# Attention and expert layer on one core: two heads for each exponential and each maximum, and attention by tokens through transpositions

## The reference

```python
qkv = x @ W_qkv.T + b_qkv                     # 32 x 256 tokens, H = 16 heads, hs = 8
att = jnp.einsum('bthd,bshd->bhts', q, k) / math.sqrt(hs)
att_prob = jax.nn.softmax(att, axis=-1)
att_v = jnp.einsum('bhts,bshd->bthd', att_prob, v)
x = _layernorm(x + att_v @ W_out.T + b_out)
...
x = _layernorm(x + _L0_ffn_ref(x, ...))       # 8 experts, top 2, and a shared one
```

## Time and profile before

| | |
|---|---|
| median of 3 runs | 873.24 us (871.66 to 875.74) |
| the profiled execution | 874.22 us, span 872.4 us |
| PE, PE weight load busy | 91%, 56% |
| DVE, ACT, POOL busy | 81%, 64%, 61% |
| mean granted TensorE clock | 0.98 |

### The profile page before, as it was taken

How to read it: one execution, slowest core, us unless ns; L and a number is a source line. 1 busy time by engine, 2 the same in 40 slices (tenths; PEclk the granted TensorE clock), 3 DMA queues, 4 the chain that set the end, 5 groups by cost and what they waited for, 6 DMA issues and landing times.

```text
span 872.4 us, 21905 instructions
## 1 busy us (share of the span) xinstructions
PE 792.0 (91%) x6356; PEld 487.8 (56%) x6356; DVE 710.5 (81%) x1430; ACT 557.5 (64%) x1128; POOL 528.2 (61%) x684
## 2 busy tenths in 40 slices
PE   2688999999999999999999689999999899999994
PEld 1234555555555555555554557666666566666662
DVE  5576988898889989889987398888888888887885
ACT  1146887777778877877778346655555555556652
POOL 3446756656657667566533357666666676666664
PEclk9997999999999999999999799999999999999997
DMA  5634555555655655555420541444444544433430
GB/s 151 187 100 117 134 167 149 144 160 134 161 145 133 177 140 133 172 137 145 135 64 27 142 120 53 121 121 122 121 120 120 120 120 120 120 115 103 121 96 24
DMA packets 201643, 108.84 MB, mean 125 GB/s; under 512 B 10496, under 2 KB 201088, under 8 KB 201600
## 3 DMA queue, kind: packets, MB, share of 16 engines
q1 hardware_dynamic: 200048, 105.88, 45.0%
q10 hardware_dynamic: 1552, 2.44, 1.0%
HBM read 73.94 MB, written 33.82 MB: 124 GB/s over the span
## 4 chain that ended last, share of the span: by engine, by line
PE 50%; DVE 16%; issue 13%; POOL 9%; DMA 7%; ACT 2%; DVEq 1%; SPq 1%; POOLq 0%; ACTq 0%
PE bank L721 11%; DVE negmax L999 8%; PE bank L693 7%; PE bank L706 6%; DMA probs<-route_dram 6%; PE bank L823 4%; PE bank L728 3%; POOL place L507 3%; PE bank L729 3%; DVE k_stack L1073 3%; PE bank L730 3%; PE bank L803 2%; POOL rstd L516 2%; PE bank L887 2%; PE bank L783 2%
## 5 line engine op out<-in xcount | busy, mean ns | idle before, releaser
L999 DVE TENSOR_REDUCE negmax<-bank 128x2 f32<-128x512 f32 x512 | 321.3, 680 | 50.5 <-PE bank L706 46.3
L555 ACT ACTIVATE probs<-bank 128x512 f32<-128x512 f32 x512 | 292.2, 604 | 94.9 <-PE bank L693 93.9
L706 PE MATMUL bank<-k_stack,q_stack 48*128 48x256 bf16 x1024 | 168.9, 284 | 12.3 <-DVE negmax L999 5.4
L693 PE MATMUL bank<-q_stack,k_stack 50*128 50x256 bf16 x1024 | 168.1, 276 | 6.0 <-ACT probs L555 4.8
L728 PE MATMUL bank<-x_hi,hi_w 128*128 128x512 f32 x288 | 137.8, 479 | 11.3 <-DVE k_stack L1073 8.6
L721 PE MATMUL bank<-probs,v_aug 128*32 128x256 f32 x2048 | 138.8, 389 | 0.4 <-ACT attT L566 0.4
L693 PEld LDWEIGHTS bank<-q_stack,k_stack 50*128 50x128 bf16 x1024 | 75.5, 95 | 98.1 <-ACT probs L555 62.7
L1063 DVE TENSOR_TENSOR k_stack<-bank,probs 128x512 f32<-128x512 f32 x128 | 87.6, 685 | 44.4 <-DMA probs<-route_dram 26.2
L729 PE MATMUL bank<-x_hi,lo_w 128*128 128x512 f32 x288 | 115.4, 401 | 0.0
L730 PE MATMUL bank<-x_lo,hi_w 128*128 128x512 f32 x288 | 115.2, 400 | 0.0
L507 POOL TENSOR_TENSOR k_stack<-k_stack,probs 128x512 f32<-128x512 f32 x48 | 62.2, 1296 | 81.2 <-DVE k_stack L1073 73.4
(11 more groups left out here) (111 smaller groups left out, 1395.4 us busy)
## 6 DMA issues: line engine op xcount, KB each, us to landing
probs<-route_dram SPq DMA_DIRECT2D x128, 256.0 KB, 5.8
q_stack<-q_parts_dram SPq DMA_DIRECT2D x64, 192.0 KB, 3.2
k_stack<-k_parts_dram SPq DMA_DIRECT2D x64, 192.0 KB, 4.0
k_parts_dram<-k_parts SPq DMA_DIRECT2D x32, 192.0 KB, 2.0
q_parts_dram<-q_parts SPq DMA_DIRECT2D x32, 192.0 KB, 2.0
xT_sb<-xT SPq DMA_DIRECT2D x32, 128.0 KB, 2.1
k_parts_dram<-k_parts SPq DMA_DIRECT2D x32, 128.0 KB, 1.9
q_parts_dram<-q_parts SPq DMA_DIRECT2D x32, 128.0 KB, 2.0
```

The lines of the kernel that those rows point to most:

```text
L555: nc.scalar.activation(probs[h][:], score_ps[BANK[h]][:].rearrange("p (j t) -> p j t", j=NT), ACT.Exp).then_inc(exp_done, 1)
L693: mm = pe.matmul(score_ps[BANK[h]][:, j * T:(j + 1) * T], k_stack[b.ring][first:last, h // 2, j * P:(j + 1) * P], q_stack[b.ring][first:la ...
L706: mm = pe.matmul(max_ps[BANK[h]][:, i * T:(i + 1) * T], q_stack[b.ring][first:last, h // 2, i * P:(i + 1) * P], k_stack[b.ring][first:last ...
L999: nc.vector.tensor_reduce(negmax[b.ring % 2][:, :, column], max_ps[BANK[h]][:].rearrange("p (i s) -> p i s", i=NT), AX_X, ALU.max, negate= ...
```

## The change

Three edits in the attention part.

1. The S scores of two neighbouring heads go to one tile of two neighbouring banks, and ACT takes one exponential of 1024 values for both heads. There is one such tile (score_ps is twos[2]), where three banks took turns before. S matmuls of a pair wait, at its first head, until the exponentials of all pairs before it are done.
2. The M scores of two neighbouring heads go to another such tile, and DVE takes one reduction of 1024 values for both. There are two such tiles, in turn; the M matmuls of a pair wait for the reduction two pairs before.
3. The four matmuls of 72 columns that turn the sums to rows by tokens become four transpositions of 128 columns. POOL builds, at the start, an identity with its columns in another order (used_first), so that the used columns come first. A later transposition writes over the unused columns of the one before it.

```diff
-        probs = [sb(f"probs{r}", [P, NT, T]) for r in range(H)]
+        two_probs = [sb(f"two_probs{r}", [P, 2, NT, T]) for r in range(PAIRS)]
+        probs = [two[:, n] for two in two_probs for n in range(2)]
...
-        max_ps, score_ps, av_ps, misc = banks[0:3], banks[3:6], banks[6], banks[7]
+        twos = [ctx.enter_context(nc.psum_tensor(f"two_banks{n}", [P, 2, 512], F32)) for n in range(3)]
+        max_ps, score_ps, av_ps, misc = twos[0:2], twos[2], banks[6], banks[7]
...
+            pool.tensor_copy(used_first[:, 0:4 * W].rearrange("p (g w) -> p g w", w=W), columns[:, :, 0:W]).then_inc(consts_set, 1)
+            pool.tensor_copy(used_first[:, 4 * W:P].rearrange("p (g w) -> p g w", g=4), columns[:, :, W:32]).then_inc(consts_set, 1)
...
-                    if b.live:
-                        act_e.wait_ge(score_mm, b.count(H, h + 1))
+                    if b.live and h % 2 == 0:
+                        act_e.wait_ge(score_mm, b.count(PAIRS, h // 2 + 1))
                         if h % 4 == 0 and b.later(1):
                             act_e.wait_ge(av_mm, b.count(4, h // 4 - 3))
-                        nc.scalar.activation(probs[h][:], score_ps[BANK[h]][:].rearrange("p (j t) -> p j t", j=NT), ACT.Exp).then_inc(exp_done, 1)
+                        nc.scalar.activation(two_probs[h // 2][:].rearrange("p h j t -> p (h j t)"), score_ps[:].rearrange("p h t -> p (h t)"),
+                                             ACT.Exp).then_inc(exp_done, 1)
...
-                if j == 0 and (b.later(1) or h >= BACK[h]):
-                    pe.wait_ge(exp_done, b.count(H, h + 1 - BACK[h]))
+                if j == 0 and h % 2 == 0 and (b.later(1) or h):
+                    pe.wait_ge(exp_done, b.count(PAIRS, h // 2))
...
-                if j == NT - 1:
+                if j == NT - 1 and h % 2:
                     mm.then_inc(score_mm, 1)
...
-                if i == 0 and (b.later(1) or h >= BACK[h]):
-                    pe.wait_ge(max_red, b.count(H, h + 1 - BACK[h]))
+                if i == 0 and h % 2 == 0 and (b.later(1) or h >= 4):
+                    pe.wait_ge(max_red, b.count(PAIRS, h // 2 - 1))
...
-                                mm = pe.matmul(tok_ps[:, (2 * i + half) * 4 * W:(2 * i + half + 1) * 4 * W],
-                                               attT[:, half, i * P:(i + 1) * P], used, start=True, stop=True)
+                                mm = pe.transpose(misc[:, first:first + P], attT[:, half, i * P:(i + 1) * P], used_first[:])
...
-                        nc.vector.tensor_reduce(negmax[b.ring % 2][:, :, column], max_ps[BANK[h]][:].rearrange("p (i s) -> p i s", i=NT),
+                        nc.vector.tensor_reduce(negmax[b.ring % 2][:].rearrange("p i (u g) -> p u i g", u=2)[:, :, :, h // 2],
+                                                max_ps[h // 2 % 2][:].rearrange("p u (i s) -> p u i s", i=NT),
                                                 AX_X, ALU.max, negate=True).then_inc(max_red, 1)
```

43 lines of the change are left out of this document (22 added, 21 removed).

## The result

| | before | after |
|---|---|---|
| median of 4 runs each, same chip | 873.76 us | 917.07 us (914.49 to 919.31) |
| ratio of after to before | | 1.0495 [1.0455, 1.0535] |
| the profiled execution, span | 874.22, 872.4 us | 918.25, 916.4 us |
| PE, DVE, ACT, POOL busy | 91, 81, 64, 61% | 86, 76, 60, 58% |

A forecast was written before the change was run, and what follows sets the result against it. PE was taken as the bound before, PE and ACT working in turn after. Full slots +32.8, others +3 and +2.5, reductions -1, transpositions -0.5: +36.8 us on 874.2, 911.0, so a median of 910 us, range 887 to 933.

The forecast's parts named there:

- the chain: In each pair of heads, S, handover, exponential and handover back follow one another: 1.80 us, between 1.67 and 1.92.
- first S to last S of a block: First link, on PE: the S matmuls of a block start within 0.35 us.
- last S to the exponential: Second link, from PE to ACT: 0.31 to 0.38 us, taken as 0.35.
- The slot: A full attention slot, eight pairs: 14.45 us against 13.28, so +32.8 us over 28 slots.
- ACT's two pieces behind pair 2: Copy of the sums and values between pairs 2 and 3 on ACT, counted as 0.05 us a slot.
- slots 0 and 1: First attention slots, partly at the low clock, whose longer matmuls cover the exponential: +2.5 us.
- slots 30 and 31: Last slots with S, without M: a chain of 1.58 us a pair, 12.65 us a slot, +3 us in all.
- the lower end of the chain: All four links of a pair at their shortest: 1.67 us, given as a slot of 13.45 us.
- The rival of the clock: Rival: PE idles in most blocks, so its clock falls to 1.2 GHz in attention; about 1030 us; 5%.
- less 1 for the reductions: In the two slots with M alone, where DVE is the bound, double reductions save 1 us.
- the cover: Rival: PE's work behind each block hides the exponential, at 0.90 us for it; not slower, about 849 us; 5%.

The follow-up runs named there:

- e5: The changed kernel with an exponential and waits for each head, on the same two banks for S; 866.60 us.
- e3: The changed kernel with each exponential cut to the first head's 512 values, the second head's probabilities left at one; 844.41 us.
- e6: The changed kernel with PE's wait for a reduction moved out of the block, ahead of its first S; 916.21 us.
- e7: The changed kernel with ACT's two waits at heads 0, 4, 8 and 12 swapped; 912.55 us.
- e9: The changed kernel with one reduction for each head again, in four banks in turn, the exponential still one for two heads; 918.10 us.
- e4: The changed kernel with the turning as before, by four matmuls of 72 columns; 926.68 us.
- e1: The kernel before with the four transpositions alone; 861.45 us.
- e10: The kernel before with the four transpositions and with S of both heads ahead of M in each block; 871.42 us.

## Why the prediction was right, and where it was off

**What bounds it.** Right. Edit 1 makes PE and ACT take turns; the profile shows both waiting, in front of 256 exponentials and the first S of nearly every block. e2 (S ahead of M, -56 us) takes the chain away with the single tile, the waits and the long exponential in place; e5 (exponential and waits by head, -50 us) and e3 (a shorter exponential, -73 us) take it away from the other side.

**The links of the chain.** Predicted 0.35 + 0.35 + 1.04 + 0.06 = 1.80, measured 0.42 + 0.31 + 1.02 + 0.06 = 1.81 in an ordinary pair. The exponential is a little cheaper (1025 ns against 597 for 512 values in e3: the further 512 cost 0.836 ns each and not 0.856); the 0.06 is exact. The Trainium skill, "ScalarE: Activation LUTs", in the step-by-step section, has 0.833 ns an element, and the trace agrees with its 0.836. Two links were mis-sized:
- *first S to last S of a block.* I took 0.35 from a block in which PE had not waited. Behind a wait, M starts 0.09 us after S, and the four pairs of matmuls are spread over 0.42. That is 8 x 0.07 = 0.56 us a slot and 16 us over 28. The cause is the register instruction ahead of M, which PE had always reached early before and now reaches only when its own wait is over: slot 0 has none, and there the spread is 0.34 as I took it; the same holds for the six looped blocks without it. e6 gives it back in 12 looped slots, and in the others takes it again ahead of S.
- *last S to the exponential.* 0.31 for most, and 0.38 at pairs 2 and 4. I took 0.35 for all, 0.18 us a slot too much. The register instruction with the late wait stands in the order rows of ACT ahead of the prediction, and I did not use it; e7 shows it to be the cause.

**The slot.** Predicted 14.45, measured 14.73 (14.83 in slots 6 to 25). The pairs of one slot add up to 14.89, and the terms to the same: 14.45 + 0.56 for the spread - 0.18 for the handover - 8 x 0.02 for the exponential, - 0.05 for ACT's two pieces behind pair 2 (pair 3 takes 1.81, so they cost nothing), + 0.19 for pair 0 and + 0.09 for pair 7, which are longer than the chain. In pair 0 the exponential starts 0.48 us after the last S, 0.17 more than elsewhere; with ACT's waits swapped in e7 it is 0.30, so it is again the late wait on the register instruction, though why it costs 0.18 here and 0.08 at pairs 2 and 4 no run shows. Behind pair 7 the first S of the next slot starts 0.14 after the exponential's end, and there it has two waits, with the late one ahead of it, as in e6. I had no term for a slot's edges. Over 28 slots it is 7.8 us more than forecast, about what the whole sum fell short by (7.2); the other stretches nearly cancel. That is in part luck: slots 0 and 1 were 1.8 us too high, slots 30 and 31 were 1.5 too low. Two roundings of the working were off by a little: the lower end of the chain gives a slot of 13.41 and not 13.45 us, and 25 below and 20 above 910 are 885 and 930.

**Slots 30 and 31.** Predicted 12.65 each, measured 13.62 and 13.38; e7, where the clock stays at 1.00, has 12.56 and 12.51. So the chain was right and the clock costs some 1.9 us (e6 and e9, at full clock in slot 30, have 12.34 there). In the changed kernel, in the stretch where the clock is 0.62:

```profile
515.57 0.60 PE L700 MATMUL two_banks<-q_stack,k_stack 50*128 50x256 bf16 x4 [1.22 <-ACT two_probs L561]
516.10 1.93 PE L728 MATMUL bank<-two_probs,v_aug 128*32 128x256 f32 x16
```

The values take 1.93 us, as at 1.2 GHz in the earlier trace rows, behind a wait of 1.22 us. Such a wait alone doesn't bring the fall: in e7's slot 30 the values behind a wait of 1.27 us take 1.07 us (510.04), and in its slot 29 those behind one of 1.26 us take 1.93 (482.67). From 140 to 440 us, where PE's waits are at most 0.8 us and PE is idle 9% of the time, the clock never fell. The rival of the clock was therefore false where it would have cost 119 us and true where it costs 2. The Trainium skill's rule on psum-queue depth-cycling ("TensorE: Matmul & The Clock Gate", the section on a second failure mode) does not agree with the full slots of this trace: the clock is 1.00 over 300 us with a pause in front of nearly every block. In slots 30 and 31 it may be what is seen; no run tells that apart.

**Slots 0 and 1.** Predicted +2.5 less 1 for the reductions, measured -0.3. The low clock covers part of the chain, and these slots, written out, have the pair of 1.73 us, shorter than any I had reckoned with.

**Edit 2.** No gain, as predicted (1.2 us for one reduction; 1.223 measured).

**Edit 3.** Four transpositions in 0.49 us (predicted 0.54). Its gain under edit 1 was to vanish: pair 4 has the chain's length, and without the edit a slot would be 0.4 longer; e4 has 0.31 (and 10 us in all). Only e1 shows what it is worth where nothing hides it, 13 us.

**The rivals.** By the prediction the cover would have held from an exponential of 0.90 us down. e3, with 0.60, is on the other side of that point and has a slot of 12.46, PE's own. What I missed is that the point moves with the spread of S as well: e2 gets there with an exponential of 1.02.

## What to carry to other kernels

A buffer that is written and read as one piece has a shortest period: the spread of the writes, the handover, the read, and the handover back (here 0.42 + 0.31 + 1.02 + 0.06). Work it out from rows before merging two instructions on a shared tile, and compare it with the writer's own work in that period: the merge costs nothing while the period is the smaller of the two. Of its terms the spread is often the one that can be cut for nothing, by putting the writes that the reader waits for ahead of what only keeps them company; but if the second of these writes has a wait of its own, as in e10, that order puts more behind the wait.

Saved busy time is no gain by itself: both merged instructions saved time on their engine (30 us of ACT's busy time from before to after, 9 of DVE's), and neither engine was the bound.
